# First-layer score maxima: the band mask moves into a TensorE matmul, and narrow query blocks of one head pair share a PSUM bank

## The reference

```
xn = layernorm(x)
q, k, v = split(xn @ w_in.T + b_in)           # 16 heads, hd = 8
scores = einsum('bhqd,bhkd->bhqk', q, k) / sqrt(8)
scores = where(abs(i - j) <= 128, scores, -1e30)
ctx = softmax(scores) @ v ; out = ctx @ w_out.T + b_out
x = x + (xn + out) + int8_quantized_ffn(xn)
# second layer: full attention with softmax over queries,
# then a mixture of 8 experts, 2 of them for each token
```

## Time and profile before

| | |
|---|---|
| time, median of 3 runs | 586.75 us (585.32 to 588.08) |
| the profiled execution: its time, its span | 585.75 us, 584.0 us |
| mean granted TensorE clock | 0.947 |
| PE busy, PEld busy | 507.6 us, 322.0 us |
| DVE, ACT, POOL busy | 440.3 us, 339.6 us, 307.3 us |
| first maximum of the first layer, last one | 30.0 us, 322.2 us |

### The profile page before, as it was taken

One profiled execution on the slowest core, in us unless ns is written; L12 is line 12 of the kernel. 1 busy time (PEld: TensorE's weight loads), 2 busy tenths in 40 slices (PEclk: granted clock), 3 DMA queues, 4 the chain that ended last, 5 costly groups with the idle time before them and its releaser, 6 DMA issues. The chain is left out here.

```text
span 584.0 us, 17179 instructions
## 1 busy us (share of the span) xinstructions
PE 507.6 (87%) x5731; PEld 322.0 (55%) x5731; DVE 440.3 (75%) x1888; ACT 339.6 (58%) x867; POOL 307.3 (53%) x361
## 2 busy tenths in 40 slices
PE   6388999998997999999989989979876999999990
PEld 5124344444443444434444547657555899999990
DVE  6698889798897987998879347899877485555652
ACT  2162777776766677777746766664463444444440
POOL 6580844825646457465020204468777376666662
PEclk9565999999999999999979999999988999999996
DMA  4847146373472644816501116211112333554424
GB/s 95 205 112 129 39 130 129 84 161 89 127 147 81 146 99 129 154 38 165 112 20 39 40 38 261 69 49 40 42 61 87 84 102 91 156 148 133 138 78 130
DMA packets 51383, 60.99 MB, mean 104 GB/s; under 512 B 10002, under 2 KB 42134, under 8 KB 49697
## 3 DMA queue, kind: packets, MB, share of 16 engines
q1 hardware_dynamic: 45824, 50.26, 35.1%
q0 software_dynamic: 4320, 8.47, 4.3%
q10 hardware_dynamic: 1152, 1.18, 0.7%
HBM read 31.68 MB, written 28.39 MB: 103 GB/s over the span
## 5 line engine op out<-in xcount | busy, mean ns | idle before, releaser
L704 DVE CUSTOM_DVE_ANT_0 A<-A,band 128x320 f32<-128x320 f32 (+2 forms) x512 | 213.3, 463 | 39.2 <-PE A L881 38.2
L881 PE MATMUL A<-Ks,Qs 48*64 48x320 bf16 (+2 forms) x1024 | 132.5, 308 | 21.0 <-DVE mneg L704 17.2
L911 PE MATMUL SB<-Qs,Ks 50*64 50x320 bf16 (+2 forms) x1024 | 132.2, 296 | 2.2 <-issue 1.3
L557 ACT ACTIVATE Pb<-SB 128x320 f32<-128x320 f32 x256 | 98.3, 441 | 38.7 <-PE SB L925 37.4
L881 PEld LDWEIGHTS A<-Ks,Qs 48*64 48x64 bf16 x1024 | 48.8, 107 | 126.9 <-DVE mneg L704 101.2
L1807 POOL DMA_INDIRECT results<-y,xt x71 | 75.9, 1068 | 45.3 <-issue 35.9
L554 ACT ACTIVATE Pb<-SB 128x384 f32<-128x384 f32 (+1 forms) x128 | 66.4, 546 | 43.6 <-PE SB L925 43.3
L1258 POOL DMA_INDIRECT expert_rows<-pay,pos x64 | 62.1, 971 | 49.4 <-DVE pay L1441 30.9
L938 PE MATMUL PV<-Pb,Va 128*32 128x320 f32 (+2 forms) x1024 | 86.3, 409 | 1.9 <-ACT Pb L554 1.6
L925 PE MATMUL SB<-ends,ident 64*64 64x128 bf16 x768 | 83.7, 220 | 0.0
L1926 PE MATMUL l_S<-xT,wt 128*128 128x128 f32 x568 | 82.1, 288 | 1.0 <-ACT xT L1815 1.0
(11 more groups left out here) (264 smaller groups left out, 844.7 us busy)
## 6 DMA issues: line engine op xcount, KB each, us to landing
Qs<-parts_dram SPq DMA_DIRECT2D x14, 384.0 KB, 5.6
Ks<-parts_dram SPq DMA_DIRECT2D x14, 384.0 KB, 9.3
xt<-expert_rows SPq DMA_DIRECT2D x71, 65.0 KB, 1.9
yb<-results SPq DMA_DIRECT2D x7, 512.0 KB, 4.3
parts_dram<-qp SPq DMA_DIRECT2D x16, 192.0 KB, 2.8
parts_dram<-kp SPq DMA_DIRECT2D x14, 192.0 KB, 2.8
xb<-in_x SPq DMA_DIRECT2D x8, 256.0 KB, 3.2
parts_dram<-qp SPq DMA_DIRECT2D x16, 128.0 KB, 2.8
```

Of the source, the lines that this page charges most:

```text
L557: act.activation(Pb[:, group % 4, c, 0:w], bank[:, 0:w], ACT.Exp).then_inc(act_exp, 1)
L704: nc.vector.tensor_tensor_reduce(scores_of, scores_of, band[:, skip:skip + w], -1.0, 3e38, ALU.add, ALU.min, mneg[:, step % 2, col:col + 1 ...
L881: mm = nc.tensor.matmul(A[k % NA_BANKS][out:out + HP, 0:w], Qs[b % RING][rows, a, HP * sub:HP * sub + HP], Ks[b % RING][rows, a, lo:lo + w ...
L911: nc.tensor.matmul(out[r0:r0 + HP, at:at + w], Ks[b % RING][rows, a, HP * sub:HP * sub + HP], Qs[b % RING][rows, a, lo:lo + w], start=not ...
```

## The change

The mask moves from VectorE to TensorE. `piece` now follows its score matmuls with a mask matmul for each half of the partitions: the bf16 identity times the two 64-column ends of `ends16`, added into the bank, as the second pass does it. `maxima` becomes a plain `tensor_reduce` with max and negation, with no second instruction and no write to PSUM.

The fills of the A banks also change. A head pair's eight blocks take six fills: blocks 0 and 7 (192 columns each) share a bank, so do blocks 1 and 6 (256 each), and blocks 2, 3, 4 and 5 have one each. A reduction of a shared bank gives two columns of `mneg`. The fills stand at slots 0, 1, 3, 4, 5 and 7 of every eight units; at slots 2 and 6 `piece` and `maxima` do nothing. A step has 24 fills, and the whole layer 384 where it had 512. In a shared bank the ends to be masked lie side by side (the end of the first block, the start of the second), so one 128-column mask matmul for each half covers them, from a third copy in `ends16`. `band` shrinks to its two ends.

```diff
+FILLS = ((0, 7), (2,), (3,), (1, 6), (4,), (5,))
+FILL_SLOTS = (0, 1, 3, 4, 5, 7)
+def fill_at(slot):
+    n = FILL_SLOTS.index(slot % NS) if slot % NS in FILL_SLOTS else None
+    return None if n is None else slot // NS * len(FILLS) + n
...
         def maxima(step, slot):
-            scores_of = A[k % NA_BANKS][:, 0:w]
-            nc.vector.tensor_tensor_reduce(scores_of, scores_of, band[:, skip:skip + w], -1.0, 3e38, ALU.add, ALU.min,
-                                           mneg[:, step % 2, col:col + 1]).then_inc(dve_max, 1)
+            if len(subs) == 2:
+                nc.vector.tensor_reduce(mneg[:, step % 2, first:last + 1:last - first],
+                                        bank[:, 0:2 * w].rearrange("p (n w) -> p n w", n=2), AX.X, ALU.max, negate=True)\
+                    .then_inc(dve_max, 1)
+            else:
+                nc.vector.tensor_reduce(mneg[:, step % 2, first:first + 1], bank[:, 0:w], AX.X, ALU.max, negate=True)\
+                    .then_inc(dve_max, 1)
...
         def piece(step, slot):
             if k >= NA_BANKS:
                 pe.wait_ge(dve_max, k - NA_BANKS + 1)
+            bank, at = A[k % NA_BANKS], 0
+            for sub in subs:
+                lo, w = reach(sub)
+                for r0 in (0, HP):
+                    rows = slice(r0, r0 + MROW)
+                    out = HP - r0
+                    nc.tensor.matmul(bank[out:out + HP, at:at + w], Qs[b % RING][rows, a, HP * sub:HP * sub + HP],
+                                     Ks[b % RING][rows, a, lo:lo + w], start=at == 0, stop=True,
+                                     skip_group_check=at > 0, tile_position=(r0, out))
+                at += w
...
+                if len(subs) == 2:
+                    ends, masks = whole[:, w - HP:w + HP], ends16[rows, 1:3, :].rearrange("p n w -> p (n w)")
+                else:
+                    ends = whole[:, 0:8 * HP].rearrange("p (n w) -> p n w", w=4 * HP)[:, :, 0:HP]
+                    masks = ends16[rows, 0:2, :]
+                mm = nc.tensor.matmul(ends, ident16[rows, rows], masks, start=False, stop=True, skip_group_check=True,
                                       tile_position=(r0, out))
             mm.then_inc(pe_A, 1)
```

More of the change, by code:

```diff
@@ L455, in _ @@
         quant_int(0)
[L456 removed]
+        pool.wait_ge(dve_const, 6)
         base_bias(0)
@@ L695, in ffn_out, with maxima @@
                                            ws_row[:], ALU.mult, ALU.mult).then_inc(dve_ffn, 1)
[L697 to L701, removed]
-            dve.wait_ge(pe_A, k + 1)
-            scores_of = A[k % NA_BANKS][:, 0:w]
-            nc.vector.tensor_tensor_reduce(scores_of, scores_of, band[:, skip:skip + w], -1.0, 3e38, ALU.add, ALU.min,
-                                           mneg[:, step % 2, col:col + 1]).then_inc(dve_max, 1)
+        def maxima(step, slot):
+            n = fill_at(slot)
+            if n is None:
+                return
+            k = STEP_FILLS * step + n
+            c, subs = n // len(FILLS), FILLS[n % len(FILLS)]
+            w, first, last = reach(subs[0])[1], NS * c + subs[0], NS * c + subs[-1]
+            dve.wait_ge(pe_A, k + 1)
+            bank = A[k % NA_BANKS]
+            if len(subs) == 2:
[5 more added lines that the diff above has]
+                    .then_inc(dve_max, 1)
         def max_parts(step):
             par = step % 2
-            dve.wait_ge(dve_max, UNITS * (step + 1))
+            dve.wait_ge(dve_max, STEP_FILLS * (step + 1))
             if step > 1:
@@ L863, in ffn_mm, with piece @@
             mm.then_inc(pe_ffn, 1)
-        def piece(step, n):
-            k = UNITS * step + n
-            c, sub = piece_of(n)
+        def piece(step, slot):
+            n = fill_at(slot)
+            if n is None:
+                return
+            k = STEP_FILLS * step + n
+            c, subs = n // len(FILLS), FILLS[n % len(FILLS)]
             b, a = step // STEPS, HG * (step % STEPS) + c
-            lo, w = reach(sub)
             if k == 0:
                 pe.wait_ge(dma_head, LOADS)
-            if k == UNITS:
+            if k == STEP_FILLS:
                 pe.wait_ge(dma_stack, LOADS)
-            if k > 0 and k % SLOTS == 0:
+            if k > 0 and k % (STEPS * STEP_FILLS) == 0:
                 pe.wait_ge(dma_stack, LOADS * (b + 1))
@@ L877, in piece @@
                 pe.wait_ge(dve_max, k - NA_BANKS + 1)
+            bank, at = A[k % NA_BANKS], 0
[8 more added lines that the diff above has]
+                at += w
             for r0 in (0, HP):
-                rows = slice(r0, r0 + MROW)
+                rows = slice(r0, r0 + HP)
                 out = HP - r0
-                mm = nc.tensor.matmul(A[k % NA_BANKS][out:out + HP, 0:w], Qs[b % RING][rows, a, HP * sub:HP * sub + HP],
-                                      Ks[b % RING][rows, a, lo:lo + w], start=True, stop=True,
+                whole = bank[out:out + HP]
+                if len(subs) == 2:
[4 more added lines that the diff above has]
+                mm = nc.tensor.matmul(ends, ident16[rows, rows], masks, start=False, stop=True, skip_group_check=True,
                                       tile_position=(r0, out))
```

28 lines of the change are left out of this document (15 added, 13 removed).

## The result

The changed kernel takes 591.96 us (median of 20 runs), the kernel before 586.69 in its 20 runs: a ratio of 1.0085, 95% interval 1.0062 to 1.0107. It is slower by 5 us, where 561 us and a gain were forecast.

The account below looks back on a forecast made before the run. VectorE was taken as the bound, with masks and ring at zero: 16 steps x 1.6 = 25.6 us off the profiled 585.75 gives 560.2, and with 1.0 for the median of the runs 561 us; range 550 to 576.

Parts of the forecast that it names:

- TensorE's 0.7 + 4.9 us of waiting for VectorE: In the 17.2 us step, first-pass matmuls and weight loads wait 5.6 us for bank releases, read as VectorE being the bound.
- 1.6 us a step: Forecast saving in each of 16 steps, cut from VectorE's 2.0 because the three engines wait for each other in more places.
- the deeper ring and the free slots: Three first-pass banks hold 1.36 us of VectorE work instead of 1.20; slots 2 and 6 don't wait on VectorE; together zero.
- The prediction's last sentence: Test of the bound: steps shorter by less than 1 us though VectorE's busy time fell would mean VectorE alone wasn't it.
- VectorE's sum: Plain reductions, 128 fewer, with lower fixed costs: VectorE saves 32 us over the layer, 2.0 us a step.
- Rival 4: Reductions from shared banks, or in this loop, have no smaller pitch than the custom operation: no gain, 587 us; chance 0.05.
- The masks at nothing: The 768 first-pass mask matmuls on TensorE go on the shorter of two parallel streams and are costed at zero.
- The 0.5 us a step that stick out: On TensorE between two attends, the second pass outlasts the first in four of eight groups; expected to be covered by waiting.
- The upper bound of the same paragraph: Masks on TensorE cost their whole pitch in every fill if they stop both streams: 384 x 0.06 = 23 us.
- Rival 2: On TensorE, scores can't start before the mask ahead has started, 3.4 us a step held up: 575 us; chance 0.12.
- Rival 3: On TensorE, each mask drains its array, 0.36 us a fill, so the kernel gets slower: 635 us; chance 0.05.
- Rival 1: TensorE and ScalarE set the pace at once; steps stop at 16.1 and 19.0 us: 566 us; chance 0.20.

Follow-up runs that it names:

- the ladder: Runs with the load in halves, ordered from the kernel before to the changed kernel, one part added at each row; sum +0.85 points of the ratio, +5 us.
- rungs two and three: On the kernel before with load in halves: plain reductions of the same 512 fills (577.86 us), then 384 wider fills without first-pass masks (568.75 us).
- the run with two banks: Changed kernel with load in halves, PSUM banks shared two for the first pass and four for the second instead of three and three: 606.14 us, 1.0335.

## Why the prediction was wrong

**What is missing from the forecast.** It was 25.6 us of gain from a faster VectorE and nothing from anything else. On the ladder the faster VectorE with its fewer fills is worth 14.8 us (rungs two and three), the masks cost 5.6, and what the load in one piece does to the longer kernel costs 14.1 (17.2 less the 3.1 that it costs the kernel before). So three terms failed: the wait that was taken for gain, the masks, and the fetch of instructions, which the prediction didn't have. The last is the largest and turns the sign.

**The first step that failed: what bounds the kernel.** The prediction took TensorE's 0.7 + 4.9 us of waiting for VectorE as time that a faster VectorE gives back, and from it came 1.6 us a step. Of the 5.6 us, 4.9 stand on the row of PEld, the weight loads. While a weight load waits for a bank, the matmuls ahead of it, `scores` and `attend` among them, can still run. Weight loads and matmuls of the kernel before, from one stretch of the step:

```profile
233.67 0.11 PEld L881 LDWEIGHTS A<-Ks,Qs 48*64 48x64 bf16 x2 [0.52 <-DVE mneg L704]
233.00 0.75 PE L938 MATMUL PV<-Pb,Va 128*32 128x320 f32 x8
233.67 0.32 PE L881 MATMUL A<-Ks,Qs 48*64 48x320 bf16 x2
```

PEld waits 0.52 us for VectorE, and PE not at all. Only the 0.7 us are matmuls that wait; by the earlier trace rows TensorE's matmuls idle for 17.20 - 15.97 = 1.2 us in that step for any reason (with modelled ends), so 5.6 us could not come back. The waits after, 233.3 to 250.0, show it from the other side (us, times, longest):

```profile
ACT Pb L563 <- PE SB L960: 2.6, 6, 0.7
DVE mneg L716 <- PE A L917: 2.4, 2, 1.3
ACT Pb L566 <- PE SB L960: 2.2, 4, 0.8
PEld A L903 <- DVE mneg L716: 1.8, 4, 0.5
PEld A L903 <- DVE mneg L720: 1.8, 4, 0.5
DVE mneg L720 <- PE A L917: 1.3, 3, 0.6
```

VectorE's own waiting went up from 2.3 to 3.7 us, while PEld's for it only fell to 3.6, and ScalarE still waits 4.8 us for TensorE (5.4 before). Both wait for TensorE's one stream. The runs put a size on it: 5.7 us gained for 22.2 us less of VectorE's time by plain reductions, 4.0 to 5.7 us lost for 22.4 us given back, and what a real wait for VectorE does is the run with two banks. The 9.1 us for fewer fills don't follow this rate; the prediction had the deeper ring and the free slots at zero within 0.3 us a step, and this rung leaves open how much of it is theirs. The prediction's last sentence named this case: steps shorter by less than 1 us though VectorE's busy time fell.

**VectorE's sum** was right: 29.7 us less busy for 32 forecast, and the pitches where nothing waits, over the layer, have medians of 0.40, 0.47 and 0.60 us for the 0.41, 0.47 and 0.61 worked out from rows 4 and 5. Rival 4 is out.

**The masks at nothing** failed too: they cost 5.6 us in the changed kernel and 7.4 on the kernel before. The 0.5 us a step that stick out are near what they cost, 0.3 to 0.4 (16.7 against 16.4, 19.8 to 20.3 against 19.4 to 19.8). But they were to be covered by TensorE's waiting, and that was the same slack which isn't there. So one misread row moved two terms. The upper bound of the same paragraph, 23 us, was not reached either.

**Rival 2** had the wrong mechanism. The timeline after, where by program order a first-pass mask stands ahead of the second pass's matmul:

```profile
243.87 0.33 PE L903 MATMUL A<-Ks,Qs 48*64 48x320 bf16 x2
243.88 0.32 PE L946 MATMUL SB<-Qs,Ks 50*64 50x320 bf16 x2
244.03 0.22 PE L917 MATMUL A<-ends,ident 64*64 64x128 bf16 x2
```

The second pass starts 0.15 us before the mask ahead of it, in the earlier trace rows it was 0.06. Rival 3, the drain with 635 us, is out with it: 768 masks cost 5.6 us and not 48.

**Rival 1**, TensorE and ScalarE setting the pace at once, was the nearest in mechanism, but its 16.1 and 19.0 us were too low: even without masks the steps stop at 16.4 and 19.4. It took ScalarE's busy time as the floor. With the exponentials halved the short step still takes 16.4. What exactly sums up to 16.4 and 19.4 (the hand-overs between `scores`, `exp` and `attend`, the fp32 blocks, the projections) is open; no run here takes it apart.

**What no rival had: the fetch of TensorE's instructions.** It decides the sign. Without it the change is worth 8 to 9 us (576.2 against 584.1 us with the load in halves; 1.56 points by the ratios), a third of the forecast but a gain. The change adds 768 matmuls, and as many weight loads, at a place where no packet of the instruction queue moves for 9.5 us beside a bulk transfer; the stock of fetched instructions, which in the kernel before ran out once by 1.3 us, now runs out three times by 3. The prediction looked at what the new matmuls do in the array and at no DMA at all, since none was moved. The Trainium skill's sentence on the fetch being mostly hidden would have confirmed it in that.

That the gap is the fetch is a reading of these facts together: nothing that the profile shows is waited for, twice there is no wait in the program, the packet starts when the load ends, and halving or cutting the load takes the gaps away in the changed kernel and leaves little to gain in the one before (3.1 and 0.8 us). Six gaps on "issue" in four kernels with the whole load (three here, one each in the kernel before, with plain maxima, and without masks) all end 1.3 to 1.5 us after the end of that packet. The order in which the DMA engines serve the queues is not shown: in the third stretch an 8 KB packet of another instruction queue, q14, did get through at 213.0. Why exactly three batches are hit was not tried.

## What to carry to other kernels

Take an engine as the bound by the waits of the matmuls themselves, not by those of the weight loads, and test it from the cheap side first: give the suspected engine more work and see whether the end moves. Before instructions are added to an engine, look in the trace for stretches in which one queue holds all DMA engines at 100% and that engine's instruction queue has no packet; cutting a bulk load of 1.5 MB there in two, issued 5 us apart, was enough here. And small matmuls that run beside others still take a place in the one stream: here 768 of them cost 4 to 7 us in each of three places.

## What the runs showed of the hardware

- Instruction fetch shares the DMA engines with data. Beside 1.6 MB in 9.5 us on q1, no 16 KB packet for TensorE moved until the load's packets had been started; TensorE then stood for 3.0 to 3.2 us, and was granted 0.60 to 0.62 of its clock for the 4.3 us after.
- The plain reduction from PSUM is cheaper than the custom operation with its read-out, at every width: medians of the pitch of 0.40, 0.33 and 0.27 us for 320, 256 and 192 columns (plain maxima, load in halves) against 0.45, 0.38 and 0.32 in the kernel before.
- Two first-pass matmuls of rows 0 to 63 and 64 to 127 start 0.01 us apart and write two partition halves of the same bank, with a second-pass matmul starting 0.01 us later in another; each is recorded at some 0.3 us, with modelled ends.
